# Loads of the down weights issued by ScalarE behind its own passes, one tile for every third chunk of gate and up

## The reference

```
def fake_quant(t, axis):                       # QMAX = 127
    s = max(max(|t|, axis) / QMAX, 1e-8)
    return clip(round(t / s), -QMAX - 1, QMAX) * s
def qlinear(x, w):                             # both quantized along the contracted axis
    return einsum('bsh,oh->bso', fake_quant(x, -1), fake_quant(w, 1))
h   = silu(qlinear(x, w_gate)) * qlinear(x, w_up)     # w_gate, w_up: 2752 x 1024
out = qlinear(h, w_down)                              # w_down: 1024 x 2752
```

## Time and profile before

| what | value |
|---|---|
| profiled execution, its own time | 1786.35 us |
| its span, first to last instruction | 1784.6 us |
| median of the three timed runs | 1786.21 us |
| mean granted clock of TensorE | 0.913 of full speed |
| busy over the span: PE, DVE, ACT, POOL | 1407.0, 1363.5, 911.0, 970.5 us |
| matmuls of gate and up (L1724), busy | 171.1 us in 704 |
| reduces of the down weights (L1855), busy | 24.2 us in 8 |

### The profile page before, as it was taken

One profiled execution on the slowest core, in us unless ns is written; L12 is line 12 of the kernel. 1 busy time (PEld: TensorE's weight loads), 2 busy tenths in 40 slices (PEclk: granted clock), 3 DMA queues, 4 the chain that ended last, 5 costly groups with the idle time before them and its releaser, 6 DMA issues. The chain is left out here.

```text
span 1784.6 us, 17613 instructions
## 1 busy us (share of the span) xinstructions
PE 1407.0 (79%) x5384; PEld 714.3 (40%) x5384; DVE 1363.5 (76%) x1642; ACT 911.0 (51%) x1314; POOL 970.5 (54%) x794
## 2 busy tenths in 40 slices
PE   6998577778779877587887887888999587677478
PEld 3433333444444444444444444443444233223233
DVE  6675899989999989999989898862674645466584
ACT  1212677677677557677676576541422234344450
POOL 0000979788789778898988888941000012122350
PEclk9999889889899989579999899999999799889699
DMA  7694343442433432436727637635710354533204
GB/s 271 215 357 177 103 130 114 162 142 95 164 139 121 134 112 94 138 109 223 255 82 251 213 110 256 224 137 186 267 48 36 83 139 92 138 92 90 63 0 165
DMA packets 155466, 264.36 MB, mean 148 GB/s; under 512 B 76560, under 2 KB 94096, under 8 KB 149552
## 3 DMA queue, kind: packets, MB, share of 16 engines
q1 hardware_dynamic: 152208, 247.54, 42.8%
q10 hardware_dynamic: 3168, 15.73, 2.3%
HBM read 207.60 MB, written 38.60 MB: 138 GB/s over the span
## 5 line engine op out<-in xcount | busy, mean ns | idle before, releaser
L1031 DVE TENSOR_TENSOR_SCAN hbuf<-decay,hbuf 128x512 f32<-128x512 f32 x512 | 612.0, 1212 | 50.3 <-ACT decay L757 50.3
L757 ACT ACTIVATE decay<-delta,chan_sb 128x512 f32<-128x512 f32 x512 | 348.6, 687 | 318.8 <-DVE hbuf L1031 317.3
L577 PE MATMUL turn<-ident,hbuf 128*128 128x128 f32 x2048 | 348.1, 301 | 205.7 <-DVE hbuf L1031 162.2
L577 PEld LDWEIGHTS turn<-ident,hbuf 128*128 128x128 f32 x2048 | 261.9, 153 | 484.6 <-DVE hbuf L1031 242.2
L1045 DVE SCALAR_TENSOR_TENSOR acc<-turn,pn,acc 128x512 f32<-128x512 f32 x360 | 263.0, 731 | 29.2 <-PE turn L577 27.8
L868 POOL TENSOR_TENSOR hbuf<-du,sx 128x512 f32<-128x512 f32 x172 | 213.1, 1275 | 2.0 <-DMA sx<-bt_scratch 2.0
L868 POOL TENSOR_TENSOR hbuf<-wout,sx 128x512 f32<-128x512 f32 x172 | 213.4, 1277 | 0.4 <-POOL wout L878 0.2
L1724 PE MATMUL bank<-codes,wout 128*128 128x512 bf16 (+1 forms) x704 | 171.1, 407 | 52.6 <-DVE gs L1868 51.6
L889 POOL TENSOR_TENSOR acc<-acc,part 128x512 f32<-128x512 f32 x120 | 153.5, 1280 | 60.2 <-ACT part L767 57.7
L1833 POOL TENSOR_TENSOR hid<-gs,us 128x512 f32<-128x512 f32 (+1 forms) x44 | 55.8, 1269 | 187.2 <-ACT gs L1792 187.2
L559 PE MATMUL bank_g<-wout,codes 128*128 128x512 f32 x256 | 138.9, 630 | 1.0 <-DVE wout L968 1.0
(11 more groups left out here) (206 smaller groups left out, 2123.2 us busy)
## 6 DMA issues: line engine op xcount, KB each, us to landing
wout<-in_woutT SPq DMA_DIRECT2D x48, 512.0 KB, 4.3
sx<-bt_scratch SPq DMA_DIRECT2D x86, 256.0 KB, 3.8
codes<-in_wg SPq DMA_DIRECT2D x8, 2048.0 KB, 8.9
ubuf<-u_scratch SPq DMA_DIRECT2D x16, 1024.0 KB, 5.8
wout<-in_w_gate SPq DMA_DIRECT2D x26, 512.0 KB, 4.4
wout<-in_w_up SPq DMA_DIRECT2D x26, 512.0 KB, 4.0
raw_d<-in_w_down SPq DMA_DIRECT2D x8, 1376.0 KB, 6.3
b_more<-bt_scratch SPq DMA_DIRECT2D x42, 256.0 KB, 3.5
```

The source lines that it names most:

```text
L577: last = pe.transpose(turn[t % 2][:, j * P:j * P + P], hbuf[:, s % 4, j, t * P:t * P + P], ident[:, :])
L757: act.activation(decay_bank[q % 2][:, :], delta[:, G % 2, j, :], ACT.Exp, scale=a_col(GD * (G % GROUPS) + j, n)).then_inc(dA_done, 1)
L1031: dve.tensor_tensor_scan(h, decay_bank[q % 2][:, :], h, 0.0, ALU.mult, ALU.add).then_inc(scan_done, 1)
```

## The change

Three things change. The load of a tile of down weights is issued by ScalarE's queue and no longer by SP's: the first ahead of ScalarE's loop, each later one right behind the third `plain_d` of the tile before. `plain_d` moves from pass c + 2 to pass c + 1, directly behind `codes_d`. And the tiles are taken up in every third pass throughout (0, 3, ..., 21), where five of them came in the passes 0, 3, 6, 9, 11 and the rest in 14, 17, 20. SP keeps `load_wT` and `turn_wd`.

```diff
-        wd_at = {c: t for t, c in enumerate((0, 3, 6, 9, 11, 14, 17, 20))}
+        wd_at = {c: t for t, c in enumerate((0, 3, 6, 9, 12, 15, 18, 21))}
@@ SP
-            def load_wd(t):
-                if t >= 1:
-                    sp.wait_ge(wd_plain, NP * t)
-                sp.dma_start(raw_d[:, :], w_down[t * P:t * P + P, :]).then_inc(wd_load, 16)
-            load_wd(0)
             for c in range(OC):
                 if c + WT < OC:
                     load_wT(c + WT)
                 if c - 2 in wd_at:
                     turn_wd(wd_at[c - 2])
-                    if wd_at[c - 2] + 1 < JT:
-                        load_wd(wd_at[c - 2] + 1)
@@ ScalarE
+            def load_wd(t):
+                if t >= 1:
+                    act.wait_ge(wd_plain, NP * t)
+                act.dma_start(raw_d[:, :], w_down[t * P:t * P + P, :]).then_inc(wd_load, 16)
+
+            load_wd(0)
             act.wait_ge(const, 3)
             for c in range(OC + 2):
 ...
                 if c - 1 in wd_at:
+                    t = wd_at[c - 1]
                     for m in range(NP):
-                        codes_d(wd_at[c - 1], m)
-                if c - 2 in wd_at:
+                        codes_d(t, m)
                     for m in range(NP):
-                        plain_d(wd_at[c - 2], m)
+                        plain_d(t, m)
+                    if t + 1 < JT:
+                        load_wd(t + 1)
```

## The result

The changed kernel takes 1763.47 us (median of four runs, 1760.79 to 1767.35) against 1785.72 us (four runs, 1784.76 to 1790.14): a ratio of 0.9872, 95% interval 0.9847 to 0.9897, so 22 us or 1.3% are gained. 1758.2 was forecast: the direction and the main mechanism were right, and by the medians the gain forecast was 6 us too large. The profiled execution is the fastest of the four (1760.79, span 1759.0).

The account below looks back on a forecast made before the run. VectorE was held up by waits for ScalarE's absolute values and the down-weight load, TensorE not the bound. Waits saved less losses, 35.2 - 2.85 - 4.2 = 28.15; 1786.35 - 28.2 = 1758.2 us, range 1754 to 1781.5.

Parts of the forecast that it names:

- The waits for the load go: VectorE's waits for the down-weight load: the seven behind the first go, 35.2 us; the first, 5.07, stays.
- the two terms that were in the sum: Losses on ScalarE: 2.85 us for `plain_d` of tile 3, no longer covered, and 4.2 us for seven load issues.
- Pass C, "5.74 + 3.32 = 9.06": Pass ending with VectorE's reduce: it starts 5.74 us in, takes 3.32 with its followers, and waits for no load.
- pass B: Pass between the one with `codes_d` and the one with the reduce; it falls from 9.14 to 6.29 us.
- The issue, 0.60: Each of seven load issues on ScalarE, ahead of the absolute value VectorE awaits, costs 0.60 us; 4.2 us together.
- The reduce beside a product: VectorE's reduce running beside GpSimd's product loses nothing: 0 and not 5.0 us.
- `plain_d` of tile 3 and pass 22: Tile 3's `plain_d` loses its cover, 2.85 us; pass 22 takes 12.28 us, 3.14 more than before.
- SP's queue, "gain nothing": SP loses eight load issues and `load_wT` moves forward, but TensorE never waited for that: no gain.
- The range of the forecast itself: With the issue 0 to 1.3 us and the reduce 0 to 0.71 longer: 1754.0 to 1766 us, chance 0.64.
- First rival, the lock: ScalarE's load issue waits for SP's issue of the turning DMA, 3.31 us more each, 1781.4 us; chance 0.22.
- Second rival: ScalarE's load issue waits behind SP's second `load_wT` transpose and the turn, 5.15 us each, 1790 us; chance 0.07.
- Third, a late landing: The load beside the turn takes over 13.1 us; at 17.3, 29 us of stall return, 1787 us; chance 0.07.

Follow-up runs that it names:

- e2: Changed kernel with `plain_d` back in pass c + 2, the load behind it still issued by ScalarE; 1754.55 us, ratio 0.9827 to the kernel before.
- e5: Changed kernel with raise_peak over only 256 of the 512 columns of each batch; 1754.22 us (one run).
- e6: Changed kernel with each GpSimd product cut into two instructions of 256 columns; 1749.18 us, ratio 0.9786 to the kernel before.
- e4: Changed kernel with the load's issue moved behind the next pass's absolute value, still on ScalarE; 1762.41 us, ratio 0.9865 to the kernel before.
- e3: Changed kernel with the load issued by SP again, behind `turn_wd`; `plain_d` stays in pass c + 1; 1762.43 us, ratio 0.9864 to the kernel before.
- e7: Changed kernel with ScalarE's six `codes_d` and `plain_d` passes spread over its gaps, load behind the second silu; 1726.97 us, ratio 0.9671 to the kernel before.
- e9: e7 with the load issued right behind the third `plain_d`, ahead of the second silu; 1726.18 us, ratio 0.9658 to the kernel before.
- e1: Changed kernel run once more without any edit; 1760.89 us, ratio 0.9863 to the kernel before.
- e11: e9 with the load issued by SP, ahead of the turning DMA in the same queue; 1727.73 us, ratio 0.9664 to the kernel before.
- e10: e9 with GpSimd's product in two instructions of 256 columns; 1706.06 us, ratio 0.9561 to the kernel before.

## Why the prediction was right, and where its size was off
- **The waits for the load go**: right; 40.3 us became 5.1, and what came in their place on ScalarE (6.5 us) are the two terms that were in the sum.
- **Pass C, "5.74 + 3.32 = 9.06"**: the step that failed. I took the start of C from a pass whose first raise_peak had been held up by `plain_d`, and so ran after GpSimd's product at 0.69. Behind a clean pass B it meets the product and takes 1.40. C is 9.67 and not 9.06 (0.71 for the raise_peak, less 0.1 by which the instructions overlap): 0.61 in each of seven tiles, 4.3 us. Both rows were on my table, the 0.69 and the 1.40, and I asked only what the product does to the reduce. e2, e5 and e6 show the mechanism: it goes with the place of `plain_d`, with the product's end, and with its cutting.
- **The issue, 0.60**: 0.5 by e4 and by the tiles of e3 (28.24 against 28.76), 0.7 us better in all. 28.2 - 4.3 + 0.7 = 24.6 against 24.5 measured.
- **The reduce beside a product**: nothing, as taken; 3.01 us. The Trainium skill (GPSIMD Engine Reference, Specifications) names instructions with two SBUF inputs as those that suffer; both operations behave so here. The same rule, applied to the raise_peak of C with the 1.40 of the earlier trace rows, would have given the missing 4.3 us.
- **`plain_d` of tile 3 and pass 22**: pass 22 is 12.25 (12.28 forecast); the 2.85 of tile 3 fits the growth of ScalarE's waits.
- **SP's queue, "gain nothing"**: right by luck. I had it become emptier by eight issues of 0.58; in fact the turn's issue grew from 3.3 to between 6.7 and 9.3 us in six tiles. It was hidden, since the transposes of gate and up behind it had to wait for TensorE anyway: the issue begun at 1477.24 ends at 1485.49, and the next transpose starts at 1489.22.
- **The range of the forecast itself**: with the issue at 1.3 us and the reduce 0.71 longer the sum gives 1768.1 and not 1766.
- **First rival, the lock**: it fell. Both issues start at 1477.24; ScalarE's takes 0.34. In e7 four took 0.36 to 0.37, each 0.52 us into an issue of SP of 7.1 to 12.2. The rule of the Trainium skill (Perfetto Trace Analysis, DMA Instruction — HWDGE), that the generator is locked for one sequencer's use until all its descriptors are made, does not agree with this, if SP's issue is taken for the time in which it holds the generator. What became long is SP's own issue, when a load is in flight beside it.
- **Second rival**: fell too. In the changed kernel SP was through with the two transposes 0.3 us before the load was issued; in e5 and e6 loads were issued inside the second transpose and took 0.33 to 0.35. **Third, a late landing**: not in the changed kernel (5.9 to 8.5 us in its two profiles), but real: 9.8 to 16.1 us for two loads of e6, three of e7 and one of e9. Its cause is open.

## What to carry to other kernels
Work of an engine that is idle half the time can still cost its full length: what matters is what waits behind it in that engine's order. Before a load is moved to another queue, look for the gap in which its consumers' passes fit; here that was worth some 34 us (e1 to e7), the earlier load some 22. And when a pass is rebuilt from rows, each operation's duration must be taken from a row with the same neighbours.

## What the runs showed that I had not expected
- VectorE's maximum over two tiles in SBUF stands until GpSimd's running product is over: 0.69 alone and 1.40 beside it, 0.42 and 1.14 at half the columns. Cutting the product in two makes it 0.86, and then GpSimd's second half stands for VectorE: its pair takes 1.86, and 1.41 beside a reduce.
- The issue of the turning DMA takes 3.3 us alone, and 6.2 to 16.1 us in the 61 cases, in eleven profiles, in which a 1376 KB load left between 1.5 us ahead of it and 0.6 us behind. It then lasts about as long as the load is in flight: it ends between 0.7 us before and 2.7 us after the landing, in the median 0.55 after. That holds in e11 too, where both stand on SP's queue (6.5 to 9.9 us). The plain load's issue on ScalarE's queue stays at 0.33 to 0.37.
- The same load on ScalarE's queue lands in 5.8 to 8.6 us in seven profiles out of ten, e10 with the fastest loop among them, and in up to 12.5, 12.4 and 16.1 us in e6, e7 and e9. Neither its order against the turn nor the loop's pace tells when.
